# Last four products with wo behind the last gate, U added by three engines, half of the semaphore clears behind the stores

## The reference

```python
h = _layernorm(x, axis=-1) * (1 + cb) + sb

def step(c, xt):
    ft = jax.nn.sigmoid(xt @ wf.T + c @ uf.T + bf)
    it = jax.nn.sigmoid(xt @ wi.T + c @ ui.T + bi)
    gt = jnp.tanh(xt @ wc.T + c @ uc.T + bc)
    c = ft * c + it * gt
    return (c, None)
c_final, _ = lax.scan(step, c0, x)
h = jnp.tanh(jnp.einsum('tbi,oi->tbo', x, wo) + c_final @ uo.T + bo)
x = x + gb * h
```

## Time and profile before

| what | value |
|---|---|
| median of 3 runs | 587.07 us (586.58 to 587.66) |
| the profiled execution, its own time | 586.33 us |
| its span, first to last instruction | 584.5 us |
| PE busy in the span | 553.9 us, 95% |
| DVE, ACT, POOL busy | 402.7, 349.3, 360.4 us |
| mean granted TensorE clock | 0.989 |

### The profile page before, as it was taken

One profiled execution on the slowest core, in us unless ns is written; L12 is line 12 of the kernel. 1 busy time (PEld: TensorE's weight loads), 2 busy tenths in 40 slices (PEclk: granted clock), 3 DMA queues, 4 the chain that ended last, 5 costly groups with the idle time before them and its releaser, 6 DMA issues. The chain is left out here.

```text
span 584.5 us, 13730 instructions
## 1 busy us (share of the span) xinstructions
PE 553.9 (95%) x4628; PEld 536.9 (92%) x4628; DVE 402.7 (69%) x1021; ACT 349.3 (60%) x873; POOL 360.4 (62%) x495
## 2 busy tenths in 40 slices
PE   6999999999988999999999999999999999999970
PEld 3899989989888999999999999999999999999960
DVE  6999999996675665566556666666566666657562
ACT  3766667777456555555665555566565566675540
POOL 4788876675365444454666666667666767676233
PEclk9999999999999999999999999999999999999995
DMA  8555444433433222222223233334233342341424
GB/s 285 150 186 177 127 126 146 132 104 99 129 111 108 64 66 87 76 72 73 73 67 116 91 95 105 103 105 139 91 91 91 95 148 85 93 125 47 90 75 144
DMA packets 58514, 64.10 MB, mean 110 GB/s; under 512 B 5408, under 2 KB 49736, under 8 KB 58448
## 3 DMA queue, kind: packets, MB, share of 16 engines
q1 hardware_dynamic: 58448, 63.26, 35.6%
HBM read 46.44 MB, written 16.81 MB: 108 GB/s over the span
## 5 line engine op out<-in xcount | busy, mean ns | idle before, releaser
L644 POOL TENSOR_TENSOR hsl<-hs,hsh 128x512 fp32r<-128x512 f32 x32 | 41.8, 1308 | 78.8 <-DVE state L1166 41.6
L1154 DVE SCALAR_TENSOR_TENSOR lo<-psT,cb1T,hi 128x256 fp32r<-128x256 f32 x64 | 28.0, 479 | 70.6 <-ACT hi L842 70.6
L1387 PE MATMUL psR<-hs,AT 128*128 128x128 f32 x432 | 62.9, 277 | 3.0 <-ACT hs L803 1.8
L635 POOL TENSOR_TENSOR hin<-hin,uvec 128x256 f32<-128x256 f32 x64 | 48.3, 776 | 28.0 <-ACT hin L786 28.0
L1387 PEld LDWEIGHTS psR<-hs,AT 128*128 128x128 f32 x432 | 54.9, 191 | 5.1 <-ACT hs L803 3.1
L897 ACT ACTIVATE psF<-psF,biasT 128x256 f32<-128x256 f32 x64 | 26.0, 445 | 45.9 <-PE psF L1424 45.9
L1063 DVE TENSOR_TENSOR pre<-psR,state 128x256 f32<-128x256 f32 x44 | 18.6, 423 | 44.3 <-PE psR L1387 44.3
L678 POOL TENSOR_TENSOR zn<-zn,tA 128x512 f32<-128x512 f32 x32 | 41.2, 1288 | 12.4 <-ACT zn L817 12.4
L817 ACT ACTIVATE zn<-state,nmA,rstdA 128x256 f32<-128x256 f32 x64 | 35.0, 594 | 20.4 <-POOL nmA L668 20.4
L1023 DVE SCALAR_TENSOR_TENSOR hin<-xin,mvA,uvec 128x256 f32<-128x256 f32 x56 | 43.4, 814 | 2.4 <-DMA h_park<-hin 0.8
L673 POOL TENSOR_TENSOR wx<-wx,tG 128x512 f32<-128x512 f32 x24 | 35.6, 1483 | 12.5 <-ACT wx L863 12.3
(11 more groups left out here) (323 smaller groups left out, 2364.0 us busy)
## 6 DMA issues: line engine op xcount, KB each, us to landing
h_park<-hin SPq DMA_DIRECT2D x32, 256.0 KB, 2.2
hin<-h_park SPq DMA_DIRECT2D x64, 128.0 KB
xin<-in_L_attn_x_dram SPq DMA_DIRECT2D x64, 128.0 KB
tA<-rows_d SPq DMA_DIRECT2D x32, 256.0 KB, 4.7
out_dram<-state SPq DMA_DIRECT2D x64, 128.0 KB
xin<-in_L_attn_x_dram SPq DMA_DIRECT2D x28, 256.0 KB, 2.9
tW<-rows_d SPq DMA_DIRECT2D x32, 128.0 KB, 4.4
tG<-rows_d SPq DMA_DIRECT2D x24, 128.0 KB, 4.4
```

The source lines that it names most:

```text
L635: pool.tensor_tensor(h, h, sa, ALU.add).then_inc(a_h, 1)
L644: pool.tensor_tensor(pair_of(hsl[:, j], t), pair_of(hs, 2 * p % 4), pair_of(hsh[:, j], t).bitcast(f32), ALU.subtract).then_inc(s_hsl, 1)
L1387: ins = pe.matmul(ps, AT[:, k, m * P:(m + 1) * P], hs[:, k, :, (t - 1) % 4, :], start=(k == 0 and (separate or m == 0)), stop=(k == H - 1 ...
```

## The change

**Products with wo.** `times_wo` of tiles 28 to 31 leaves the units and stands in PE's `last_outputs`: that of tile 28 ahead of the products that make U, that of 29 behind them, those of 30 and 31 between the additions of U. The shift row `tW` is no longer added behind the product: DVE copies it into the bank ahead of it (tiles 28 to 30), or PE lays it there with a product by `ident` (tile 31), and `times_wo` adds to what is there. Since the split tokens `hi` and `lo` have two places each, those of tiles 30 and 31 go to the places of `hsh` and `hsl`, no longer used then (`split_of`).

**U.** Its second half is made in psT instead of psG, and the four products stand by k, not by half. DVE adds U to tiles 25 and 27 from its bank, POOL adds `uvec` to tiles 24 and 26, and PE adds it to 28 to 31 as before. Tile 31 is finished in two halves, the left on DVE and the right on POOL, with a tanh each.

**SP.** The flag is read ahead of the wait for U. 25 of the 50 clears stay ahead of the stores, 25 go behind them, and the stores come in another order. (psC and psO also get one start flag for a whole bank, with no instruction more or less.)

```diff
--- before.py
+++ after.py
-    ON_POOL = (LAST, LAST + 2, NU - 1)
+
+    ON_POOL = (LAST, LAST + 2)
     HELD = NU - 4
-    TANHS = (LAST + 1, LAST, LAST + 3, LAST + 2, *range(HELD, NU))
-    STORES = (LAST + 1, LAST, LAST + 3, LAST + 4, LAST + 2, LAST + 5, LAST + 6, LAST + 7)
+    ON_DVE = (LAST + 1, LAST + 3, HELD, HELD + 1, HELD + 2)
+    STORES = (LAST + 1, LAST + 3, HELD, LAST, HELD + 1, HELD + 2, LAST + 2)
+    TANHS = (LAST + 1, LAST + 3, LAST, HELD, LAST + 2, HELD + 1, HELD + 2)
...
-            return wx[:, o % NWX, :] if o < HELD else (psC, psR, psO, psW)[o - HELD][:, :]
+            return wx[:, o % NWX, :] if o < HELD else (psC, psO, psW, psR)[o - HELD][:, :]
...
-            return {LAST + 1: psF, LAST + 3: psI}[o][:, :] if o < HELD else sum_of(o)
+            return {LAST + 1: psI, LAST + 3: psG}[o][:, :] if o < HELD else sum_of(o)
+
+        def split_of(n, few, state_of):
+
+            if n < NU - 2:
+                return few[:, n % 2, :, :]
+            i = (n - NU + 2) * H * POS
+            return state_of[:, 0].rearrange("p m b t k -> p (m b t k)")[:, i:i + H * POS].rearrange("p (k n) -> p k n", k=H)
...
-                sp.wait_ge(s_Ul, 2)
-                clear(of_middle)
                 sp.wait_ge(k_flag, 1)
                 sp.reg_mov(left, sp.value_load(again[0:1, 0:1], min_val=0, max_val=K))
+                sp.wait_ge(s_Ul, 2)
+                half = len(of_middle) // 2
+                clear(of_middle[0:half])
                 for o in STORES:
                     store(o)
+                for j, done, n in ((0, s_fin, LAST + len(ON_DVE) + 1), (1, s_fp, len(ON_POOL) + 1)):
+                    sp.wait_ge(done, n)
+                    sp.dma_start(out_t[(NU - 1) % NB, steps(NU - 1, j), :, :], tiles_of(NU - 1)[:, j, :]).then_inc(s_out, 16)
+                clear(of_middle[half:])
 
                 sp.wait_ge(r_over, r * 4 + 4)
...
             def last_outputs():
+                pool.wait_ge(s_u, NT + 1)
+                for o in ON_POOL:
+                    pool.tensor_tensor(sum_of(o), sum_of(o), uvec[:, :], ALU.add).then_inc(s_up, 1)
                 pool.wait_ge(s_tL, 16 * 4)
...
+                t = wx[:, (NU - 1) % NWX, D:W]
+                pool.wait_ge(s_ot, LAST + len(TANHS) + 1)
+                pool.tensor_tensor(t, t, gb_of(NU - 1), ALU.mult).then_inc(s_ob, 1)
+                pool.wait_ge(s_ob, LAST + len(ON_POOL) + 1)
+                pool.tensor_tensor(tiles_of(NU - 1)[:, 1, :], t, tiles_of(NU - 1)[:, 1, :], ALU.add).then_inc(s_fp, 1)
...
-                for j, src in enumerate((psF, psG)):
+                for j, src in enumerate((psF, psT)):
                     act.wait_ge(s_Ul, j + 1)
                     act.activation(uvec[:, j * D:(j + 1) * D], src[:, 0:D], ACT.Copy).then_inc(s_u, 1)
...
-                    dve.wait_ge(s_W, n + 1)
-                    dve.wait_ge(s_tW[n % 2], 16 * (n // 2 + 1))
-                    dve.tensor_tensor(two(sum_of(n)), two(sum_of(n) if n >= HELD else psW[:, :]), both(tW[:, n % 2, :]), ALU.add).then_inc(s_wx, 1)
+                    if n < HELD:
+                        dve.wait_ge(s_W, n + 1)
+                        dve.wait_ge(s_tW[n % 2], 16 * (n // 2 + 1))
+                        dve.tensor_tensor(two(sum_of(n)), two(psW[:, :]), both(tW[:, n % 2, :]), ALU.add).then_inc(s_wx, 1)
+                    elif n < NU - 1:
...
+                        dve.wait_ge(s_tW[n % 2], 16 * (n // 2 + 1))
+                        dve.tensor_copy(two(sum_of(n)), both(tW[:, n % 2, :])).then_inc(s_wx, 1)
...
-                for j in range(2):
-                    dve.wait_ge(s_u, NT + j)
-                    half = slice(j * D, (j + 1) * D)
-                    for o in TANHS[0:4]:
-                        last = dve.tensor_tensor(tanh_of(o)[:, half], uvec[:, half], sum_of(o)[:, half], ALU.add)
-                        if j:
-                            last.then_inc(s_uz, 1)
+                for o in ON_DVE[0:2]:
+                    for j, u in enumerate((psF, psT)):
+                        dve.wait_ge(s_u, NT + j)
+                        half = slice(j * D, (j + 1) * D)
+                        last = dve.tensor_tensor(tanh_of(o)[:, half], u[:, 0:D], sum_of(o)[:, half], ALU.add)
+                    last.then_inc(s_uz, 1)
...
-                if x:
+                if x and n < HELD:
                     times_wo(n)
...
+            def add_u(o):
+                for j in range(2):
+                    if o == HELD:
+                        pe.wait_ge(s_u, NT + j)
+                    last = pe.matmul(sum_of(o)[:, j * D:(j + 1) * D], ident[:, :], uvec[:, j * D:(j + 1) * D],
+                                     start=False, stop=True, skip_group_check=True)
+                last.then_inc(s_ub, 1)
+
             def last_outputs():
-                for j, dst in enumerate((psF, psG)):
-                    for k in range(H):
-                        pe.wait_ge(s_cl, k + 1)
-                        last = pe.matmul(dst[:, 0:D], cst[:, k, j * P:(j + 1) * P], uoT[:, k, :], start=(k == 0), stop=(k == H - 1))
-                    last.then_inc(s_Ul, 1)
-                pe.wait_ge(s_wx, NU)
...
+                times_wo(HELD)
+                for k in range(H):
+                    pe.wait_ge(s_cl, k + 1)
+                    for j, dst in enumerate((psF, psT)):
+                        last = pe.matmul(dst[:, 0:D], cst[:, k, j * P:(j + 1) * P], uoT[:, k, :],
+                                         start=(k == 0), stop=(k == H - 1), skip_group_check=True)
+                        if k == H - 1:
+                            last.then_inc(s_Ul, 1)
+                times_wo(HELD + 1)
+                add_u(HELD)
+                add_u(HELD + 1)
+                times_wo(HELD + 2)
+                add_u(HELD + 2)
                 for j in range(2):
...
+                    pe.matmul(psR[:, j * D:(j + 1) * D], ident[:, :], tW[:, (NU - 1) % 2, :], start=(j == 0), stop=False,
+                              skip_group_check=True)
+                times_wo(NU - 1)
+                add_u(NU - 1)
```

More of the change, by code:

```diff
@@ L302, in adaln_kernel @@
         s_uz = sem("s_uz")
+        s_up = sem("s_up")
         s_ub = sem("s_ub")
@@ L521, in store @@
                 else:
-                    sp.wait_ge(s_fin, LAST + len([i for i in range(LAST, o + 1) if i not in ON_POOL]))
+                    sp.wait_ge(s_fin, LAST + ON_DVE.index(o) + 1)
                 for j in range(2):
@@ L838, in hi_of @@
                     act.wait_ge(q_cb, 2)
-                if n >= 2:
+                if n >= NU - 2:
+                    act.wait_ge(s_C, len(CSEQ))
+                elif n >= 2:
                     act.wait_ge(s_W, n - 1)
                 for k in range(H):
-                    act.activation(hi[:, n % 2, k, :], psT[:, k * POS:(k + 1) * POS], ACT.Copy,
+                    act.activation(hi_at(n)[:, k, :], psT[:, k * POS:(k + 1) * POS], ACT.Copy,
                                    scale=cb1T[:, k, n % NB:n % NB + 1]).then_inc(s_hi, 1)
@@ L1206, in last_outputs @@
             def last_outputs():
-                for j in range(2):
-                    dve.wait_ge(s_u, NT + j)
-                    half = slice(j * D, (j + 1) * D)
-                    for o in TANHS[0:4]:
-                        last = dve.tensor_tensor(tanh_of(o)[:, half], uvec[:, half], sum_of(o)[:, half], ALU.add)
-                        if j:
-                            last.then_inc(s_uz, 1)
+                for o in ON_DVE[0:2]:
[4 more added lines that the diff above has]
+                    last.then_inc(s_uz, 1)
                 dve.wait_ge(s_tL, 16 * 4)
-                for i, o in enumerate(o for o in range(LAST, NU) if o not in ON_POOL):
+                for i, o in enumerate(ON_DVE):
                     t = two(tanh_of(o))
@@ L1220, in last_outputs @@
                     dve.tensor_tensor(tiles_of(o), t, tiles_of(o), ALU.add).then_inc(s_fin, 1)
+                t = psR[:, 0:D]
+                dve.wait_ge(s_ot, LAST + len(TANHS) + 2)
+                dve.tensor_tensor(t, t, gb_of(NU - 1), ALU.mult).then_inc(s_oz, 1)
+                dve.wait_ge(s_oz, len(ON_DVE) + 1)
+                dve.tensor_tensor(tiles_of(NU - 1)[:, 0, :], t, tiles_of(NU - 1)[:, 0, :], ALU.add).then_inc(s_fin, 1)
             def body():
@@ L1413, in project @@
                             last = pe.matmul(ps[:, i * D:(i + 1) * D], h[:, j, k, b + i, :, :].rearrange("p t k -> p (t k)"), w["C"][:, k, :],
-                                             start=(n == 1), stop=(n == 3 * H))
+                                             start=(n == 1 and i == 0), stop=(n == 3 * H), skip_group_check=True)
                 if end == 2:
@@ L1440, in gate_x @@
                     pe.wait_ge((s_fc, s_c, s_g)[i], (n, n, 2 * n)[i])
-                last = split3((psF, psI, psG)[i], ("wf", "wi", "wc")[i], hi[:, n % 2, :, :], lo[:, n % 2, :, :], True, n % NB == 0)
```

(9 more changed lines are left out.)

52 lines of the change are left out of this document (31 added, 21 removed).

## The result

| | changed kernel | kernel before |
|---|---|---|
| median of 5 runs | 582.02 us (581.56 to 583.72) | 586.58 us (586.04 to 587.66) |
| ratio, 95% interval | 0.9924 (0.9905 to 0.9942) | |
| profiled execution, span | 581.56, 579.7 us | 586.33, 584.5 us |
| mean granted TensorE clock | 0.994 | 0.989 |

A forecast was written before the change was run, and what follows sets the result against it. PE was taken to set the pace until tile 31's gates, then SP's store queue. Gates -3.66 and clears -1.58 made -5.24 us, from 587.07 to 581.8 us; own range 581.0 to 582.5, 8-in-10 range 580.4 to 583.3.

The forecast's parts named there:

- Part 1: Gates of tiles 28 to 31: wo products leave four units; of 6.0 us, 3.7 arrive.
- T(31): Start of tile 31's c products (T(n): tile n's): forecast at 552.96, 3.66 us earlier.
- Unit 38: PE up to tile 29's c products: idles for `gf`, small waits of 0.2 us go; start 534.85, 1.7 us earlier.
- Unit 39: PE from tile 30's first product to its c products: 4.56 us; start 544.45, 2.24 us earlier.
- Unit 41: PE from tile 30's c products to tile 31's, no norm left: 8.51 us; start 552.96, 3.66 us earlier.
- Part 2: From the last gate to tile 23's store: nothing changed between; tile 23 ready at 560.8, 3.66 us earlier.
- Part 3: SP's queue: 25 clears fewer ahead of the first store save 1.58 us; flag exchange worth nothing; moved clears hidden by landing.
- Part 4: Data behind the last gate arrive in time for SP's stores; least margin 0.45 us, at the first store.
- Swallowed gates: Rival, chance 0.17: `gf` loop of units 38 and 39 swallows both gains; -4.4 us in all, 582.7 us.
- Data instead of SP: Rival, chance 0.07: tile 25 about 1.3 us late, or tile 31 3 us late, so SP waits; -3.9, 583.2 us.
- Half clock: Rival, chance 0.04: PE at half clock behind the last gate, 11.7 us of work becoming 23.4; slower, 589.9 us.
- Stores landing ahead of the clears: Rival, chance 0.04: transfers keep up with issue, queue of clears sets the end, 0.5 us earlier; 581.3 us.

The follow-up runs named there:

- more_pe_ahead_of_31: Changed kernel with 24 more wo products between the addition of U to tile 30 and the row of tile 31: 582.67 us, ratio to before 0.9924.
- all_clears_ahead: Changed kernel with all 50 clears ahead of the 16 stores again: 584.25 us, ratio to before 0.9951.
- split_alone: Kernel before with only the clears split, 25 ahead of the 16 stores and 25 behind: 585.88 us, ratio to before 0.9983.
- all_clears_behind: Changed kernel with all 50 clears behind the 16 stores: 582.04 us, ratio to before 0.9922.
- flag_and_clears_in_gap: Changed kernel with flag load and 37 clears between the stores of tiles 22 and 23, 13 clears behind the 16 stores: 580.38 us, ratio to before 0.9899.
- pair of leave-outs: Kernel before with 8 of 12 wo products left out, for tile 28 alone (586.42 us, ratio 1.0002) or tile 31 alone (585.90 us, 0.9988).
- changed_again: Changed kernel measured and profiled once more, no edit: 582.97 us, ratio to before 0.9928.
- its three variants: Kernel before with the clears split (0.9983), or with 8 wo products left out for tile 28 (1.0002) or tile 31 (0.9988).
- before_less_wo_28: Kernel before with 8 of the 12 wo products left out for tile 28 alone: 586.42 us, ratio to before 1.0002.

## Why the prediction was right

**What bounds the end.** SP's queue, not data, in the kernels before and changed: more_pe_ahead_of_31 adds 2.8 us to the last tile for nothing, all_clears_ahead adds 25 clears to the queue for their full price. Where SP comes earlier, in split_alone, all_clears_behind and flag_and_clears_in_gap, tile 25's data release the first store. Behind the first store both kernels take the same, 14.6 and 14.5 us to the end of the span. Whether the pace of the issues or the transfers' rate sets that stretch (183 to 191 GB/s in the full slices of either) no run separates, since both begin with the first store.

**Part 1, the gates.** The mechanism is confirmed by the pair of leave-outs: PE time taken from tile 28's unit is swallowed by `gf`, PE time taken from tile 31's arrives at T(31). The size was off. 3.66 us were forecast at T(31), and 3.24 came in the first profile, 3.0 to 3.5 over the profiles with the gates of before (40.40 to 40.65) and of after (37.16 to 37.44). Three terms make the missing 0.42.

- Unit 38. The forecast took 0.2 us of small waits of PE off the stretch between the wait for `gf` and T(29). None lay in it: it was 536.54 - 530.36 - 1.50 = 4.68 before and is 534.54 - 529.87 = 4.67 after. The 0.17 at T(29) pass through the transposes and `gf` to tile 30's first product, 24.09 behind T(27) for a forecast of 23.92.
- Unit 39. The stretch was forecast at 4.56 and took 4.67. Its products start 118 ns apart throughout, while in the kernel before two groups of twelve stood 113 apart. That is of the execution and not of the change: in changed_again the two stretches take 4.55 and 4.54, and T(29) is 18.94 and T(30) 28.51, close to the forecast. The kernel before varies in the same way, with T(29) at 20.57 in its own profile and 20.42 or 20.43 in its three variants.
- Unit 41. T(31) lies 8.65 to 8.67 behind T(30) in all six profiles of the changed gates, not 8.51. 0.08 of it is in the first two c products of tile 30: the second starts 0.20 behind the first (544.25, 544.45), where behind a group with wo it was 0.12 (546.69 before). So a group taken out brings 1.42 in the end and not the 1.50 that was counted from the rows. The other 0.06 is not traced further.

**Part 2** held: tile 23 is ready 7.8 us behind T(31) in the changed kernel (560.72 - 552.90) as before (564.45 - 556.62).

**Part 3, SP.** The term of 1.58 us brought 1.3. The 63 ns were a mean over a run with a pause in it. The same clears in two parts, the kernel before and then the changed one:

```profile
L471 SPq EVENT_SEMAPHORE_RANGE_CLEAR  x18: 25/25/40, 565.8 to 566.8; - x18
L471 SPq EVENT_SEMAPHORE_RANGE_CLEAR  x32: 25/25/31, 567.2 to 568.9; - x32
...
L487 SPq EVENT_SEMAPHORE_RANGE_CLEAR  x14: 25/25/40, 563.4 to 564.2; - x14
L487 SPq EVENT_SEMAPHORE_RANGE_CLEAR  x11: 25/25/31, 564.6 to 565.2; - x11
```

The clears start 55 ns apart, and one pause of 0.4 us stands among those ahead of the stores, whether they are 25 or 50. It stays there when 25 are moved, so these bring 1.3 to 1.4. The exchange of the flag's load with the wait was taken as free and cost 0.36: the load is 845 ns instead of 489. In the four other profiles where it stands right behind tile 23's stores it takes 823 to 943, in the four where it stands behind clears (the kernel before and its three variants) 488 or 489. -1.3 + 0.36 = -0.94: between the end of tile 23's stores and the first of the group lie 4.17 us before (565.73 to 569.90) and 3.22 now (562.00 to 565.22). The load's price is read from its rows; no run has the exchange alone.

**Part 4, data in time.** Counted from T(27), tile 25 was ready at 48.4 for a forecast of 48.2, and SP came at 49.7 for a forecast of 48.7, so the margin was 1.3 us instead of 0.45.

**The sum.** -3.24 - 0.94 = -4.2, beside -4.3 in the last column and -4.5 by the ratio; -5.24 had been worked out. The landing hides the 25 moved clears with 0.5 us to spare, as worked out, and all_clears_behind shows where that cover ends.

**The rivals.** Swallowed gates: true of unit 38; unit 39 paid partly, and 3.24 lies between this rival's 2.84 and the forecast's 3.66. Data instead of SP: excluded for the first store by the 1.3 us for which tile 25 lies ready, and for the last tile by more_pe_ahead_of_31. Half clock: excluded by the granted clock. Stores landing ahead of the clears: by the fixed and the variable cost in the Trainium skill (DMA: Bandwidth & Descriptors, Anatomy of one DMA), fitted to DMAs issued from GpSimd, the estimate is 2.3 us from the last issue's start. Here 3.8 us pass from it (575.4) to the end of the wait (579.2), and the wait for landing is still there. The measurement decides, for this queue of 16 stores behind each other.

## What to carry to other kernels

Where PE is busy without a gap, look for the loops through other engines that lie just under its pace, and ask of each unit which of them ends next: two units here had one (the norm's), two had none, and the same edit reached T(31) with nothing from one and with its full time from the other. At a kernel's end, draw the store queue first: work ahead of its first store costs its full time, work behind its last is free as long as the landing takes, and work on the last tile is free as long as the queue behind it. Small bookkeeping of a queue (clears, a register load) belongs where that queue waits.

## What was not expected of the hardware

- The same products of PE, at a granted clock of 1.00, start 113 to 114 ns apart in one execution and 118 apart in the next, for up to 36 products: from the first product behind the wait for `gf` to the transposes pass 4.32 us in one profile of the changed kernel and 4.19 or 4.17 in the other. The slow steps were seen to begin behind a stall of 0.1 to 1.4 us, but not every stall brings them (in before_less_wo_28 a wait of 0.95 us is followed by steps of 113 to 114 within a few products). What decides it, no run here shows.
- The load of one word into a register of SP takes 0.49 us behind a run of clears, and 0.82 to 1.08 us elsewhere. Where the time goes was not tried.
- Clearing semaphores one by one is 25 ns each by the row and 55 ns from one to the next. Among those ahead of the stores stands one pause of 0.4 us, behind the 18th clear in the kernel before and its variants and, where the four steps of the flag's load come between tile 23's stores and the clears, behind the 14th: behind the same number of SP's instructions. The clears behind the stores have none. So it goes with the place in SP's program and not with the number of clears; what it is stays open.
